# A transformer tower on one core: the sequence experts and the block attention put into one stage, piece by piece

## The chip, the cores and the metric

One core of a Trainium2 chip runs the whole program. The metric is the device time of one execution in microseconds; the median of three runs stands for a kernel. The engines are TensorE (PE), VectorE (DVE), ScalarE (ACT), GpSimd (POOL) and SyncE (SP), each with its own instruction queue that is worked off in order.

## What is computed

Eight images of 1024 tokens, 128 channels wide, pass five layers. Each adds its output to the stream `h`:

```python
h = tok(x, W) + positions
h = h + attention(layernorm(h))                 # 8 heads, softmax over 1024 keys
h = h + sequence_experts(layernorm(h))          # 2 of 8 experts for a whole image
h = h + block_attention(layernorm(h))           # below
h = h + token_experts(layernorm(h))             # 2 of 8 experts for each token

def sequence_experts(x):                        # g: gates from a pooled image, two are not 0
    h = gelu(einsum('bsd,edh->ebsh', x, w1) + b1)
    eo = gelu(einsum('ebsh,eho->ebso', h, w2) + b2)
    return einsum('ebso,be->bso', eo, g)

def block_attention(x):                         # 32 blocks of 32 tokens; all blocks are in the band
    q, k, v = x @ W_qkv + b_qkv
    attn = softmax(einsum('bisc,bjsc->bisj', qb, kb) * scale)
    out = einsum('bisj,bjsc->bisc', attn, vb)
    return out @ W_proj + b_proj
```

Block attention is within an image, and so is the gate of an image in the sequence experts. The token experts need the counts of all tokens of all images before they start.

## The kernel before

`tower` runs five blocks one after the other, with a barrier between two: `embed_and_attend` (the first two layers, 0 to 632 us of the profile), `sequence_experts` (632 to 844), `block_attention` (844 to 1155), `token_experts` (1155 to 1425), `add_results`. The stream H stays in SBUF. Between the last two the rows go through DRAM: `send` (L1580) writes the normalised rows into a queue sorted by expert.

**`sequence_experts`** (helper `expert_items`). An image takes four tiles: two halves of 512 tokens, each with two experts; 32 tiles in all. A tile has four parts n. `first` makes a hidden part in PSUM (three matmuls of 512 columns, L70 to L72, the operands split into two fp32r parts). ACT's `hidden` reads it twice with Gelu (L1192 into `g_hi`, L1195 into `g`), DVE's `low` takes the rest (L1288), `second` adds the part into `psY`. After four parts ACT's `output` makes `y` (L1208), `turn_y` transposes it into `psT` (L1257), DVE's `back` adds it to H by the gate. PE's order is `first(m + 1, n)`, then `second(m, n)`, with `turn_y(m - 1)` after n = 2. `turn_x` transposes the tokens of a new half (L1227) into `psX`, ACT (L1202) and DVE split it. All eight PSUM banks are in use: four `psH`, two `psY`, `psX`, `psT`. The class `Rest` puts what is left of the second layer and of the gates between these parts, up to tile 16. SP loads the weights of the experts.

**`block_attention`** takes image after image, over all five engines: DVE statistics and `apply_x`, PE `turn` (L1694), ACT `places` and `first_bits`, DVE `split_x`, PE `project` (L70 to L72), `values` (L1719), `scores` (L1729), DVE `shift`, ACT Exp, DVE `weights`, PE `attend` (L1741), ACT `attended`, PE `output` (L1747 to L1751), DVE `add`, statistics (L130), POOL root (L1573), `apply_z` (L141), PE `turn_z` (L1701), ACT `copy_z`, PE `logits` (L1759), DVE `choose` (two highest of 8, L1862 to L1878), PE `positions` (L1766 to L1769), DVE `route` (L1884 to L1898), POOL 16 sends. Parts of image b + 1 stand between those of b. It too uses eight banks, one or two for each purpose. After the last image comes `plan`: the counts, the tiles of each expert, the padding of the queue, four loads of weights; then the token experts' first rows are read.

## Time and profile before

| | |
|---|---|
| median of 3 runs | 1419.37 us (1413.64 to 1426.13) |
| span of the profiled execution | 1475.5 us |
| busy over the span | PE 1206.2 us (82%), ACT 994.0 (67%), DVE 932.3 (63%), POOL 557.8 (38%) |
| mean granted clock of TensorE | 0.889 |
| sequence experts | 632 to 844 us |
| block attention and plan | 844 to 1158 us |

A row of a timeline gives the start, the time (of all that a row merges), the engine, line and operation, output and inputs, how many, and in brackets how long the engine had been idle and for what. "remote" and "issue" mean that the profile shows nothing that ended the wait. Two instructions that follow each other overlap, so the cost of one is read from start to start. The clock is given in parts of the full one; 0.5 is 1.2 GHz and 1.0 is 2.4 GHz.

### The profile page before, as it was taken

The numbers are of one execution on the slowest core, as the hardware profiler recorded it, in microseconds if no ns is written. First come the engines' busy times: TensorE is split into PE (matmuls) and PEld (weight loads), VectorE is DVE, ScalarE is ACT, GpSimd is POOL, SyncE is SP. The second block draws the span as 40 slices with busy tenths as digits, with TensorE's granted clock in tenths as the row PEclk, the third lists the DMA queues.
The fourth block names the chain that finished last, engine by engine and source line by source line (L and its number), as shares of the span: only waits on it lengthen the run. The fifth ranks groups of instructions, "written<-read, shape, count | busy, mean of one in ns | idle before, by whom it ended". The sixth has DMA issues, their size and how long they took to land. (4 is left out here: it accounts for less than half of the span.)

```text
span 1475.5 us, 26945 instructions
## 1 busy us (share of the span) xinstructions
PE 1206.2 (82%) x9386; PEld 808.9 (55%) x9386; DVE 932.3 (63%) x2604; ACT 994.0 (67%) x1348; POOL 557.8 (38%) x538
## 2 busy tenths in 40 slices
PE   3699999999999998889999867877661599999950
PEld 2344444444444443477788656766451487888740
DVE  4366877777787877578676667776242266666535
ACT  0498888888888888688799744434110489999840
POOL 3423333343434332101000012667526067777660
PEclk9799999999999999899999968787555799999975
DMA  3573828282927372232122000111103467777619
GB/s 89 107 180 92 198 86 200 80 185 83 203 86 182 96 168 64 64 129 86 58 100 73 8 4 7 41 37 45 38 17 129 175 220 238 245 237 240 217 44 341
DMA packets 93162, 180.56 MB, mean 122 GB/s; under 512 B 15597, under 2 KB 64200, under 8 KB 84960
## 3 DMA queue, kind: packets, MB, share of 16 engines
q1 hardware_dynamic: 72832, 129.18, 31.3%
q0 software_dynamic: 17344, 42.68, 8.9%
q10 hardware_dynamic: 2848, 6.95, 1.7%
q8 instruction: 76, 1.25, 0.4%
q14 instruction: 62, 0.51, 0.1%
HBM read 116.96 MB, written 63.12 MB: 122 GB/s over the span
## 5 line engine op out<-in xcount | busy, mean ns | idle before, releaser
L777 ACT ACTIVATE a_probs<-a_psS 128x1024 f32<-128x1024 f32 x512 | 484.1, 1034 | 86.5 <-PE a_psS L862 53.0
L874 PE MATMUL a_psO<-a_probs,a_v 128*32 128x256 f32 x4096 | 281.6, 393 | 17.2 <-DVE a_o_t L1051 16.8
L1288 DVE TENSOR_TENSOR f_g_lo<-f_g,f_g_hi 128x512 fp32r<-128x512 f32 x284 | 194.7, 689 | 149.7 <-ACT f_g L1195 108.7
L2024 POOL DMA_INDIRECT result<-f_out,f_idx x156 | 181.4, 1163 | 107.0 <-issue 61.3
L874 PEld LDWEIGHTS a_psO<-a_probs,a_v 128*32 128x32 f32 x4096 | 108.5, 110 | 153.8 <-issue 88.8
L1580 POOL DMA_INDIRECT queue<-all_row,all_idx x128 | 125.1, 977 | 42.0 <-issue 36.9
L1192 ACT ACTIVATE f_g_hi<-f_psH,all_w 128x512 fp32r<-128x512 f32 x156 | 109.3, 701 | 24.5 <-PE f_psH L72 19.7
L1195 ACT ACTIVATE f_g<-f_psH,all_w 128x512 f32<-128x512 f32 x156 | 109.3, 701 | 0.0
L862 PE MATMUL a_psS<-ag_qs,ag_ks 50*128 50x512 f32 x512 | 97.0, 455 | 13.2 <-DMA ag_qs<-a_gparts 6.6
L862 PE MATMUL a_psS<-a_qs,a_ks 50*128 50x512 f32 x512 | 97.5, 457 | 7.7 <-issue 3.1
L438 POOL TENSOR_TENSOR ag_rs_f<-ag_veps_f,all_half 128x4 f32<-128x4 f32 x32 | 33.8, 1055 | 128.4 <-DVE ag_veps_f L135 128.4
L1202 ACT ACTIVATE f_x_hi<-f_psX 128x512 fp32r<-128x512 f32 x55 | 33.1, 602 | 59.5 <-PE f_psX L1227 59.5
L862 PEld LDWEIGHTS a_psS<-ag_qs,ag_ks 50*128 50x128 f32 x512 | 39.7, 190 | 60.9 <-ACT a_probs L777 31.0
L862 PEld LDWEIGHTS a_psS<-a_qs,a_ks 50*128 50x128 f32 x512 | 39.8, 191 | 54.9 <-ACT a_probs L777 36.7
L70 PE MATMUL f_psH<-f_x_hi,all_w 128*128 128x512 f32 x156 | 68.5, 439 | 0.0
L72 PE MATMUL f_psH<-f_x_hi,all_w 128*128 128x512 f32 x156 | 62.0, 398 | 0.0
L71 PE MATMUL f_psH<-f_x_lo,all_w 128*128 128x512 f32 x156 | 62.0, 397 | 0.0
L70 PE MATMUL f_psY<-f_g_hi,all_w 128*128 128x512 f32 x156 | 61.6, 395 | 0.0
L72 PE MATMUL f_psY<-f_g_hi,all_w 128*128 128x512 f32 x156 | 61.4, 394 | 0.0
L71 PE MATMUL f_psY<-f_g_lo,all_w 128*128 128x512 f32 x156 | 61.4, 394 | 0.0
L746 POOL DMA_DIRECT2D experts<-a_split x32 | 19.7, 615 | 107.9 <-DVE a_split L1069 107.9
L1192 ACT ACTIVATE f_g_hi<-f_psH,f_w 128x512 fp32r<-128x512 f32 x64 | 44.6, 697 | 15.1 <-PE f_psH L72 14.7
(368 smaller groups left out, 2660.0 us busy)
## 6 DMA issues: line engine op xcount, KB each, us to landing
all_w<-experts SPq DMA_DIRECT2D x39, 1026.5 KB
experts<-a_split POOLq DMA_DIRECT2D x32, 512.0 KB, 5.0
f_rows<-queue SPq DMA_DIRECT2D x39, 260.0 KB
f_w<-experts SPq DMA_DIRECT2D x8, 1026.5 KB, 5.3
qparts<-a_parts SPq DMA_DIRECT2D x16, 512.0 KB, 4.2
kparts<-a_parts SPq DMA_DIRECT2D x14, 512.0 KB, 3.3
ag_qs<-experts SPq DMA_DIRECT2D x4, 1026.5 KB, 5.1
ag_ks<-experts SPq DMA_DIRECT2D x4, 1026.5 KB, 4.8
```

The lines of the kernel that those rows point to most:

```text
L70: nc.tensor.matmul(out, w_lo, x_hi, start=first, stop=False)
L71: nc.tensor.matmul(out, w_hi, x_lo, start=False, stop=False)
L72: return nc.tensor.matmul(out, w_hi, x_hi, start=False, stop=last)
L438: self.nc.gpsimd.tensor_tensor(self.rs_f[:, :], self.veps_f[:, :], half[:, 0:TPC], ALU.pow).then_inc(self.root_f, 1)
L777: nc.scalar.activation(probs[u % NPR][:, :], psS[score_buffer(u)][:, :, :].rearrange("p a n -> p (a n)"), ACT.Exp).then_inc(exp_done, 1)
L862: last = nc.tensor.matmul(psS[score_buffer(u)][:, p, :], ks[par][64 * p:64 * p + KG, kt, hp * P:(hp + 1) * P], queries(par, hp, p, a), sta ...
L874: last = nc.tensor.matmul(psO[32 * g:32 * g + 32, a * HALF:(a + 1) * HALF], v[par][:, 2 * hp + p, kt, :], probs[u % NPR][:, cols:cols + HA ...
L1192: nc.scalar.activation(g_hi[i][:, n, :], psH[n][:, :], ACT.Gelu, bias=bias(m, n))
L1195: nc.scalar.activation(g[:, n, :], psH[n][:, :], ACT.Gelu, bias=bias(m, n)).then_inc(g_done, 1)
L1288: nc.vector.tensor_tensor(g_lo[i][:, n, :], g[:, n, :], g_hi[i][:, n, :].bitcast(F32), ALU.subtract).then_inc(lo_done, 1)
L1580: pool.indirect_dma_start(queue, bass.IndirectOffsetOnAxis(ap=idx[n % NROW][:, k, t:t + 1], axis=0), row[n % NROW][:, k, t, :], None).then ...
L2024: pool.indirect_dma_start(result, bass.IndirectOffsetOnAxis(ap=idx[i][:, j:j + 1], axis=0), out[i][:, j, :], None, bounds_check=2 * B * S ...
```

## The change

The two stages become one, `experts_and_blocks`. It counts steps: step s is part n = s mod 4 of tile m = s div 4, 16 steps to an image, 128 steps with expert work and 42 behind them. The tables of `Blocks` say at which step after the end of image b's tiles each engine does each piece of b's attention; a number in a table counts from step 16(b + 1). So pieces of three images are in flight, and in one turn of 16 steps PE meets `positions` (of b - 2), `attend`, `output` (b - 1), `turn` (b), `turn_z` (b - 1), `values`, `project0` (b), `logits` (b - 1), `project1`, `scores` (b).

PSUM is shared out anew: three `psH`, one `psY`, one `psT` (for x, y and `Rest` alike), and three banks `psB` for the attention, which go round: each use takes the bank of the use three before it and waits (`into`, `FREED`) until that one's reader is done. `turn_y` moves to n = 1. `g` is cut from four parts to three.

Smaller parts: the softmax weight of the routing is made by POOL (`route_power`), not by ACT; the copy of the rows is a DMA on SP's queue, not an activation; the bias of `output` takes one matmul of 33 rows, not two; `positions` runs in bf16; the queue's rows have two buffers, not three; SP issues the attention's constants between the expert loads. ACT's Exp (`power`) now stands among Gelus.

```diff
+class Blocks:
+    PE = {8: "turn", 10: "values", 11: "project0", 12: "project1", 13: "scores", 17: "attend", 19: "output", 26: "turn_z", 28: "logits",
+          32: "positions"}
+    ACT = {8: "places", 9: "first_bits", 10: "values", 11: "queries_keys0", 12: "queries_keys1", 14: "power", 17: "attended0", 18: "attended1",
+           26: "copy_z0", 27: "copy_z1"}
+    DVE = {3: "moments_x0", 4: "moments_x1", 6: "apply_x0", 7: "apply_x1", 9: "split_x", 14: "shift", 15: "weights", 20: "add", 21: "moments_z0",
+           22: "moments_z1", 24: "apply_z0", 25: "apply_z1", 29: "choose0", 30: "choose1", 33: "route"}
+    POOL = {5: "root_x", 23: "root_z", 31: "route_power", 34: "send0", 35: "send1", 36: "send2", 37: "send3", 38: "send4", 39: "send5", 40: "send6",
+            41: "send7"}
+    SP = {26: "copy_rows"}
+    BANKED = {"turn": ("x0", "x1"), "values": ("v0", "v1"), "project0": ("q0", "k0"), "project1": ("q1", "k1"), "scores": ("s",),
+              "attend": ("a0", "a1"), "output": ("p0", "p1"), "turn_z": ("z0", "z1"), "logits": ("l",), "positions": ("r",)}
+    STEPS = 42
+    def __init__(self, B):
+        self.B, self.end = B, 16 * B + self.STEPS
+        self.uses = [(b, name) for s in range(self.end) for b, piece in self.at(self.PE, s) for name in self.BANKED[piece]]
+        self.place = {use: u for u, use in enumerate(self.uses)}
+    def at(self, table, s):
+        return [(b, table[s - 16 * (b + 1)]) for b in range(self.B) if s - 16 * (b + 1) in table]
...
-def sequence_experts(nc, H, ident, half, mean1, rstd1, score1, gate, chosen, shared, parts, ins, B, S, D):
...
-def block_attention(nc, H, queue, counts, row, idx, sent, tile_e, tile_row, parts, w1, w1_in, ident, half, ins, B, S, D):
...
+def experts_and_blocks(nc, H, ident, half, mean1, rstd1, score1, gate, chosen, shared, experts, w, w1_in, queue, tile_e, tile_row, ins, B, S, D):
...
+    NG, NH, NBANK = 3, 3, 3
...
+        psH = [c.ps(f"psH{i}", [P, CH]) for i in range(NH)]
+        psY, psT = c.ps("psY", [P, CH]), c.ps("psT", [P, CH])
...
+        psB = [a.ps(f"psB{i}", [P, CH]) for i in range(NBANK)]
...
+        def bank(b, name):
+            return psB[plan_of.place[b, name] % NBANK]
...
+            def copy_rows(b):
+                sp.wait_ge(zn_done, b + 1)
+                sp.dma_start(row[b % NROW][:, 1, :, 0:D], row[b % NROW][:, 0, :, 0:D]).then_inc(row_in[b % NROW], 16)
...
+            copy_rows(0)
+            load_parts(4)
+            copy_rows(1)
             shared.spread_gates(sp, 1, gate, chosen)
             load_parts(5)
             sp.wait_ge(shared.gate_in, 64)
             for b in range(6, B):
+                copy_rows(b - 4)
                 load_parts(b)
+            for b in range(B - 4, B):
+                copy_rows(b)
...
+            sp.wait_ge(planned, 1)
+            sp.wait_ge(y_done, M)
+            for i in range(len(w)):
+                e = sp.value_load(tile_e[0:1, i:i + 1], min_val=0, max_val=E - 1)
+                sp.dma_start(w[i], experts[1][bass.ds(e, 1), :, :].rearrange("o p c -> p (o c)")).then_inc(w1_in[i], 16)
...
+            def send(b, lo, hi):
+                pool.wait_ge(slot_done, b + 1)
+                pool.wait_ge(row_in[b % NROW], (b // NROW + 1) * 16)
...
+                elif name == "route_power":
+                    pool.wait_ge(gap_done, b + 1)
+                    nc.gpsimd.tensor_tensor(ex[:, :], shared.base[:, 0:T], gap[:, :], ALU.pow).then_inc(ex_done, 1)
...
+            def hidden(m, n):
+                i, u = m % 2, m * NB + n
+                if n == 0:
+                    w_wait(act, m)
+                act.wait_ge(h_ps, u + 1)
+                if n == 0 and m >= 2:
+                    act.wait_ge(y_ps, m - 1)
+                nc.scalar.activation(g_hi[i][:, n, :], psH[u % NH][:, :], ACT.Gelu, bias=bias(m, n))
+                if u >= NG:
+                    act.wait_ge(lo_done, u - NG + 1)
+                nc.scalar.activation(g[u % NG][:, :], psH[u % NH][:, :], ACT.Gelu, bias=bias(m, n)).then_inc(g_done, 1)
...
+            def output(m):
+                act.wait_ge(y_ps, m + 1)
+                if m >= 2:
+                    act.wait_ge(t_ps, m - 1)
+                nc.scalar.activation(y[m % 2][:, :], psY[:, :], ACT.Gelu, bias=bias(m, NB)).then_inc(y_done, 1)
...
+                elif name == "power":
+                    act.wait_ge(sub_done, b + 1)
+                    nc.scalar.activation(pr, sc, ACT.Exp, scale=SCALE).then_inc(exp_done, 1)
...
+            for s in range(END):
+                m, n = divmod(s, NB)
+                if s == 0:
+                    act.wait_ge(c_in, C_IN)
+                if m + 1 < M:
+                    hidden(m + 1, n)
+                if n == 0 and m % K == 0 and m + K < M:
+                    token_bits((m + K) // K)
+                for b, name in plan_of.at(Blocks.ACT, s):
+                    piece(name, b)
+                if n == NB - 1 and m < M:
+                    output(m)
...
+            def first(m, n):
+                j, u = m // K, m * NB + n
+                if n == 0:
+                    w_wait(pe, m)
+                    pe.wait_ge(x_done, j + 1)
+                if u >= NH:
+                    pe.wait_ge(g_done, u - NH + 1)
+                hi, lo = first_parts(m, n)
+                product(nc, psH[u % NH][:, :], hi, lo, x_hi[j % 2], x_lo[j % 2]).then_inc(h_ps, 1)
+            def second(m, n):
+                i = m % 2
+                if n == 0 and m:
+                    pe.wait_ge(y_done, m)
+                pe.wait_ge(lo_done, m * NB + (n + 1))
+                hi, lo = second_parts(m, n)
+                last = product(nc, psY[:, :], hi, lo, g_hi[i][:, n, :], g_lo[i][:, n, :], first=(n == 0), last=(n == NB - 1))
+                if n == NB - 1:
+                    last.then_inc(y_ps, 1)
...
+            def turn_y(m):
+                pe.wait_ge(y_done, m + 1)
+                for i in range(TPC):
+                    last = nc.tensor.transpose(psT[:, i * P:(i + 1) * P], y[m % 2][:, i * P:(i + 1) * P], ident[:, :])
+                last.then_inc(t_ps, 1)
+            FREED = {"x": (xt_done, 2), "v": (v_done, 2), "q": (qk_done, 4), "k": (qk_done, 4), "s": (sub_done, 1), "a": (o_done, 2),
+                     "p": (h_done, 2), "z": (z_done, 2), "l": (sel_done, 1), "r": (slot_done, 1)}
+            def into(b, name):
+                u = plan_of.place[b, name]
+                if u >= NBANK:
+                    was, old = plan_of.uses[u - NBANK]
+                    done, each = FREED[old[0]]
+                    part = int(old[1:] or 0)
+                    pe.wait_ge(done, was * each + {"q": 2 * part + 1, "k": 2 * part + 2}.get(old[0], part + 1))
+                return psB[u % NBANK]
...
+                        out = into(b, f"p{h}")
+                        nc.tensor.matmul(out[:, :], ones_r[:, :], b_two[:, :], start=True, stop=False)
...
+                    nc.tensor.matmul(out[:, 0:TE], before[:, :], both[:, :, :], start=True, stop=False)
+                    nc.tensor.matmul(out[:, 0:TE], all_ones[:, :], counts_b[:, :].unsqueeze(1).broadcast_to([P, T, E]), start=False, stop=False)
+                    for d in range(1, T):
+                        last = nc.tensor.matmul(out[:, d * E:TE], all_ones[:, :], both[:, 0:T - d, :], start=False, stop=(d == T - 1))
...
+            for s in range(END):
+                m, n = divmod(s, NB)
+                more = m % K == 0 and m + K < M
+                if s == 16:
+                    pe.wait_ge(ready, 1)
+                    pe.wait_ge(cleared, 1)
+                if n == 0 and more:
+                    if m >= 2:
+                        pe.wait_ge(t_read, m - 1)
+                    else:
+                        pe.wait_ge(x_done, 1)
+                    turn_x((m + K) // K)
+                if m + 1 < M:
+                    first(m + 1, n)
+                for b, name in plan_of.at(Blocks.PE, s):
+                    piece(name, b)
+                if m < M:
+                    second(m, n)
+                if n == 0 and m in Rest.PE:
+                    if more:
+                        pe.wait_ge(x_done, (m + K) // K + 1)
+                    else:
+                        pe.wait_ge(t_read, m - 1)
+                    Rest.pe(shared, pe, m, psT)
+                if n == 1 and 1 <= m <= M:
+                    if m in Rest.PE:
+                        pe.wait_ge(freed, sum(m >= i for i in Rest.PE))
+                    elif more:
+                        pe.wait_ge(x_done, (m + K) // K + 1)
+                    elif m >= 2:
+                        pe.wait_ge(t_read, m - 1)
+                    else:
+                        pe.wait_ge(freed, 1)
+                    turn_y(m - 1)
+            pe.wait_ge(slot_done, B)
+            nc.tensor.matmul(psY[:, 0:E], all_ones[:, :], counts_b[:, :], start=True, stop=True).then_inc(n_ps, 1)
+        @block.vector
+        def _(dve):
...
+            def low(u):
+                m, n = divmod(u, NB)
+                i = m % 2
+                dve.wait_ge(g_done, u + 1)
+                nc.vector.tensor_tensor(g_lo[i][:, n, :], g[u % NG][:, :], g_hi[i][:, n, :].bitcast(F32), ALU.subtract).then_inc(lo_done, 1)
...
+            for s in range(END):
+                m, n = divmod(s, NB)
+                if s + 3 < M * NB:
+                    low(s + 3)
+                if n == 0 and m % 2 and (m + 3) // K < M // K:
+                    rows_next((m + 3) // K)
+                if n == 1 and m % K == 0 and m + K < M:
+                    token_rest((m + K) // K)
+                if (m, n) == (1, 2):
+                    constants()
+                rest.dve(dve, m, n)
+                for b, name in plan_of.at(Blocks.DVE, s):
+                    piece(name, b)
+                if n == 2 and 1 <= m <= M:
+                    back(m - 1)
             plan()
```

## Rows read from the trace of the kernel before

**Rows 1.** windows: stretch, us, busy us of PE, PEld, DVE, ACT, POOL; clock; DMA

```profile
641.00:844.00 203.00, 196.17 (x933) 157.97 (x931) 148.41 (x326) 174.66 (x292) 7.91 (x4) 0.99 0.19 63
...
720.00:730.00 10.00, 9.32 (x38) 7.10 (x37) 5.13 (x11) 6.62 (x11) 0.00 (x0) 0.83 0.00 2
...
966.00:993.00 27.00, 20.61 (x179) 17.75 (x179) 19.98 (x90) 11.15 (x18) 19.86 (x19) 0.81 0.12 40
```

**Rows 2.** timeline of ACT in the expert stage: start us, us, engine line op

```profile
746.08 0.69 ACT L1208 ACTIVATE f_y<-f_psY,f_w 128x512 f32<-128x512 f32 x1
...
746.81 0.69 ACT L1192 ACTIVATE f_g_hi<-f_psH,ag_ks 128x512 fp32r<-128x512 f32 x1
...
747.96 0.61 ACT L1202 ACTIVATE f_x_hi<-f_psX 128x512 fp32r<-128x512 f32 x1
...
760.46 0.61 ACT L1202 ACTIVATE f_x_hi<-f_psX 128x512 fp32r<-128x512 f32 x1
```

**Rows 3.** timeline of PE in the expert stage: one gap, first, second

```profile
718.63 0.38 PE L272 MATMUL f_psT<-ag_corr,ag_ones 128*128 128x2 f32 x2 [2.83 <-DVE all_H L1472]
...
747.26 0.40 PE L70 MATMUL f_psH<-f_x_hi,ag_ks 128*128 128x512 f32 x1
...
747.96 0.39 PE L70 MATMUL f_psY<-f_g_hi,ag_qs 128*128 128x512 f32 x1
```

**Rows 4.** timeline of PE in one attention batch at the full clock

```profile
957.87 0.49 PE L1747 MATMUL a_psO<-a_b_lo,a_ones_r 1*128 1x512 f32 x1
...
959.52 0.33 PE L1766 MATMUL a_psR<-a_both,a_before 128*128 128x64 f32 x2
...
961.45 0.48 PE L70 MATMUL a_psQ<-a_x_hi,a_w_lo 128*128 128x512 f32 x1
...
962.92 1.95 PE L1719 MATMUL a_psX<-a_w_v,a_xT 128*128 128x128 f32 x16
...
965.14 0.76 PE L1729 MATMUL a_psS<-a_k,a_q 128*32 128x32 f32 x64 [0.27 <-ACT a_k L1630]
...
965.83 1.09 PE L1694 MATMUL a_psX<-all_ident,a_f 128*128 128x128 f32 x8
```

**Rows 5.** timeline of DVE in attention: choice, half of apply, statistics

```profile
935.38 1.64 DVE L130 BATCH_NORM_STATS2 a_stat_z<-all_H 128x6 f32<-128x128 f32 x8
...
951.92 0.22 DVE L1862 TENSOR_REDUCE a_top<-a_left 128x8 f32<-128x64 f32 x1
...
953.40 0.29 DVE L1875 TENSOR_TENSOR a_both<-a_sel 128x64 f32<-128x64 f32 x1
...
954.04 1.11 DVE L141 TENSOR_SCALAR a_f<-all_H,a_mv_x,a_rs_x 128x128 f32<-128x128 f32 x4
```

**Rows 6.** timeline of POOL in attention: root, and one send

```profile
964.97 1.67 POOL L1573 TENSOR_TENSOR a_rs_z<-a_veps_z,all_half 128x8 f32<-128x8 f32 x1 [2.91 <-DVE a_veps_z L135]
...
968.24 0.96 POOL L1580 DMA_INDIRECT queue<-all_row,all_idx  x1 [0.31 <-issue]
```

**Rows 7.** timeline of ACT where its function set changes

```profile
1162.93 1.28 ACT L1192 ACT_TABLE_LOAD   x1 [0.73 <-PE f_psH L72]
...
1164.22 0.69 ACT L1192 ACTIVATE f_g_hi<-f_psH,all_w 128x512 fp32r<-128x512 f32 x1
```

**Rows 8.** timelines of PE and DVE, last attention batch to token experts

```profile
1055.26 0.56 PE L1729 MATMUL a_psS<-a_k,a_q 128*32 128x32 f32 x40
...
1074.13 0.42 DVE L1829 TENSOR_REDUCE a_mx<-a_psS 128x8 f32<-128x256 f32 x1 [20.86 <-remote]
...
1101.93 3.58 PE L1759 MATMUL a_psR<-a_w_r,a_zT 128*128 128x8 f32 x16 [0.69 <-ACT a_zT L1619]
...
1110.00 3.10 PE L1769 MATMUL a_psR<-a_both,a_all_ones 128*128 128x56 f32 x14
...
1124.32 0.23 DVE L1886 TENSOR_TENSOR a_pos<-a_psR,a_base 128x64 f32<-128x64 f32 x1 [14.76 <-remote]
...
1157.85 0.48 PE L1227 MATMUL f_psX<-all_ident,f_rows 128*128 128x128 f32 x1 [31.35 <-DMA f_rows<-queue]
```

916 lines of the change are left out of this document (428 added, 488 removed).

## The prediction

> **What bounds the kernel now.** The page comes first: no engine is busy all through, so the stages have to be read apart. The windows show the expert stage as PE's: 196 of 203 us at clock 0.99, ACT behind it with 175 [rows 1]. ACT's timeline gives its beat: two tiles from one `f_x_hi` to the next but one, 747.96 to 760.46, 12.5 us, 6.25 for a tile [rows 2]. An attention batch is the opposite: 27 us in which PE has 20.6, DVE 20.0, POOL 19.9 and ACT 11.2, at clock 0.81 [rows 1]; none is full, and each waits for the next one. Side by side the two kinds of work would fill each other's gaps.
>
> I go by one stretch, from 641 us (the tiles run) to 1157.85, the first matmul of the token experts [rows 8]: 517 us. Two holes in it belong to no work. DVE waits 20.86 us until 1074.13 for scores that began at 1055.26 and elsewhere take 0.76 for all 64 [rows 4, 8]: some 18 us. It waits until 1124.32 for `positions`, whose last matmul ends at 1113.1: 11.2 us. Both are marked "remote". The profiled span is 56 us over the median of the runs; I take it that these 29 us are part of that and that the timed runs don't have them. Their stretch is then 488 us.
>
> **What PE has to do in one turn of 16 steps.** Four tiles: 25.0 us. The pieces at the full clock, start to start [rows 4]: `turn` and `turn_z` 1.09 each; `values` 1.95; `attend` and `logits`, sixteen passes over the same weights' size, 1.9 each; four products of `project` 2 x 1.47; `scores` 0.76; `output` 2 x 1.65, less one bias matmul of 0.32 in each, 2.7; `positions` 1.93 in fp32, in bf16 some 1.0 (the trace has no bf16 one; between a quarter and all of it, 0.5 to 1.9). Sum 15.3, with the tiles 40.3 us. DVE: 148 us over 32 tiles are at most 4.6 a tile, and less without what `Rest` does, some 16 a turn [rows 1]; with 20.0 for attention 36. ACT: 175/8 + 11 = 33 and two changes of function set. POOL: sixteen sends of 1.27 and two roots of 1.67, 24 [rows 6]. So PE stays the engine with most to do, with 4 us over DVE.
>
> **What the order and the banks add.** A turn written out by hand, each engine in its queue's order, prices: `first` and `second` 0.70 each [rows 3], `hidden` 1.15, `output` 0.6, `low` 0.6, half an `apply` 1.1, statistics of a half 0.8, the rest of them 0.9 [rows 2, 5]. PE then stops at these places:
>
> - Step 3, `output` waits for `attended1`, which stands behind `hidden` of step 2: 1.0.
> - Step 8, `turn_x` waits for `back` and `turn` for `apply_x1`. DVE has `add`, 1.7 of statistics, 0.9, 1.7, two halves of apply, four `low`, `rows_next` (1.1) and `back` between step 4 and 7, 10 us from the last `output` on, PE 7.5: 2.2.
> - Step 9, `turn_y` shares `psT` with `turn_x` and waits until DVE has split x. DVE's `apply_z0` waits for `root_z`, which POOL reaches after six pairs of sends (15.2 us) and `root_x`: 1.7.
> - Step 11, `q0` gets the bank of `z1`. `copy_z1` comes on ACT after `hidden`, whose `first` PE has just done: 1.15 + 0.5 + 0.15 = 1.8.
> - Step 13, `scores` gets the bank of `logits`, free when `choose1` has made `both`. DVE has `low(s + 3)` ahead of `choose1`, and that needs the hidden part of this very step. After `first`: 1.15 + 0.6 + 1.8 (951.92 to 953.69 [rows 5]) + 0.3 of handing over = 3.8. Earlier the bank had a reader of its own.
> - Step 16, `second` waits for `y`, now in one bank. ACT has the Exp between: a load of 1.28 us, Exp 0.4, a load of 1.28 [rows 7], `hidden`, `output`. That is 6.0 after `first` of step 14 and PE has 4.0 to do: 2.0.
>
> Sum 12.5. 40.3 + 12.5 = 52.8, say 53 us a turn. Handing over from one engine to the next is an estimate, 0.1 to 0.15 each time; at nothing the turn would be 51, at 0.25 it would be 55.
>
> The clock. A gap of 2.83 us at 718.6 left a slow stretch in a stage that is else at 0.99 (0.83 over the 10 us from 720 [rows 1, 3]): 10 x 0.17 / 0.5 = 3.4 us at 1.2 GHz, 1.7 us lost. The gap at step 13 is longer. From nothing to one such loss for each of three gaps (5): I take 1. Turn: 54.
>
> One rule of the Trainium skill speaks against the change more than my rows do. Its page "ScalarE: Activation LUTs", section "What ACT_TABLE_LOAD costs", puts a switch at 1283 ns of load and some 1380 ns of drain, 2.66 us. The trace agrees on the 1283; at 1162.93 the next activation begins right behind the load, but ACT had been idle before it, so no drain could show [rows 7]. By the page two switches cost 5.3 us and not 2.6, the stop at step 16 would be 4.8 long, and the sum below 22 us higher, by estimate.
>
> **The other parts.** Tiles 0 to 3 have no attention, but every `second` with n = 0 waits for `y` of the tile before in one bank: `hidden` 1.15 and `output` 0.6 against `second` and `first`, 1.4, with handing over 0.7 a tile: 4 x 6.95 = 28. The next turn has only the pieces up to `scores` (6.7): 25 + 6.7 + three such waits, 2, + the Exp, 2 = 36. The third has no sends, so no stop at step 9: 51. Five full ones (steps 48 to 127): 270. `Rest` on one `psT`, with its additions on DVE up to tile 16: 4.
>
> Behind step 127 the last image's attention runs alone with what is left of the two before it, and PE at half clock (sixteen passes 3.58 [rows 8] for 1.95). Chain: the last `back`, `positions` and `route` of image 5, 5; four pairs of its sends 10.1 and `root_x` 1.7, at 17; meanwhile apply and turn of image 7, but `split_x` stands behind `apply_z` of image 6, whose root stands behind four more sends: 27.5; `turn_z`, `values` 5.5, `project0` 2.6, `logits` 3.6, `project1` 2.6, `scores` 1.5 and some waits for banks: 44.5; shift, load, Exp, weights 5.5: 50; `attend` 3.8, `attended` 1.1, `output` 5, `add` and statistics 3.5: 63.5, but `root_z` stands behind twelve sends of image 6, that start at 52 after `route`, so 69; apply 2.2, turn 2, copy 0.6, `logits` 3.6, `choose` 4.1, `positions` 2, `route` 2: 85.5. From `route` to the first token matmul before: 1125.8 to 1157.85, 32 (sixteen sends 20, landing, four loads of weights, rows). The same code follows: 32. Together 118.
>
> The last parts at nothing: the constants' DMAs and `constants` have SP and DVE free in the first tiles (if not, 3 us of landing once); ACT's copy of the rows goes to a DMA that is used 8 steps later; the expert loads wait on tiles of 10 us more than the transfer needs; two row buffers are enough, as the sends of b - 2 end 15 steps before `apply_z(b)`; POOL's `route_power` (about 1.7, by its roots) is needed two steps later. The barrier between the stages, 1 us, goes.
>
> Sum: 28 + 36 + 51 + 270 + 4 + 118 = 507, against 517 in the profile and 488 without the holes. The profiled execution: 1475.5 - 10 = 1466. The timed runs: 1419.4 + 19 = **1438 us**.
>
> **The rivals.**
> - *The hand order holds, but the holes are in the timed runs too and go away.* For it: the profile has them. Against: the span is 56 us longer than the runs. 1438 - 29 = 1409.
> - *The other side: PE's queue hardly stops, and the stage is bound by its work.* Mechanism: DVE and ACT run ahead, so that each piece is ready when PE comes. For it: 40.3 of work on the fullest engine, and in attention no engine is over 76% busy [rows 1], so each has room to run ahead. Against: the stops at 11, 13 and 16 are in the order itself, not in how busy an engine is. It decides at a turn of 50.5 us (19 us over five and a half turns less). At 42 to 46 with a tail of 110: 1438 - 8 x 5.5 .. - 12 x 5.5 - 8, 1386 to 1364. The Trainium skill's page "Perfetto Trace Analysis", section "Optimization Strategy", says that interleaving regimes in which different engines are fullest may gain; the windows show two such regimes [rows 1].
> - *The stops take the clock.* Three gaps of 2 us or more in 53: if PE is at half speed for a third of a turn, five to seven us are added, by the 718.6 gap's 1.7 for each and longer ones as in attention, where the clock is 0.81. 1438 + 6 x 5.5 = 1471.
> - *A change of function set costs more than its load, because ACT has to run empty first.* For it: in the one row ACT was idle before the load, so a cost of that kind could not show [rows 7]. Against: nothing in the trace has it. At most as much again as the load, 1.3 each time, twice a turn, on the path of step 16: 8 x 2.6 = 21, 1459. The Trainium skill's page named above ("ScalarE: Activation LUTs") states such a drain.
>
> **How the numbers follow.** The forecast has 0.42, the holes' rival 0.13, PE-bound 0.27, the clock 0.13, the function sets 0.05. The range leaves out the lower end of PE-bound and half of the clock's: 1366 to 1470. The likeliest's own is 1420 to 1456. Within 1% (1405 to 1434), about what a measurement of this kernel can tell, falls the lower third of the forecast and most of the second; faster by over 1% is PE-bound and a little of the second, 0.31; same 0.22; slower 0.47.
>
> **What the profile would show.** Turns of 53 to 54 us between two `project0`; PE idle 3.8 before `scores` with DVE's `choose` as releaser, 1.8 before `q0` for ACT; two table loads a turn; the token experts 118 us after the last expert matmul at a clock of 0.5. No idle before `scores`, or turns below 50, would make the forecast wrong; a mean clock under 0.9 in the turns speaks for the last rival.

## The result

The changed kernel takes 1482.7 us (median of four runs, 1480.2 to 1498.4) against 1416.5 for the kernel before beside it: ratio 1.048, 95% interval 1.042 to 1.054. With both timed again on another chip it was 1497.3 against 1421.9, ratio 1.049 (1.044 to 1.055). The forecast was 1438 us.

The profiled executions have to be set side by side with care. That of the changed kernel has a span of 1481.8 us and took 1483.9, so it is like its timed runs. That of the kernel before was 1475.5 where its runs take 1417. A second profiled execution of the kernel before, the first experiment below, has 1417.4; it is the one to compare with. All times below are counted between the starts of three matmuls: the first `first` product of the expert stage, the last expert matmul, and the first matmul of the token experts.

| us | before, first profile | before, second profile | after |
|---|---|---|---|
| first expert product starts at | 631.3 | 629.3 | 623.5 |
| from there to the score projection of `Rest` | 6.4 | 6.4 | 15.6 |
| on to the last expert matmul | 204.1 | 204.1 | 419.7 |
| on to the first token matmul | 316.0 | 264.9 | 110.3 |
| the whole stretch | 526.5 | 475.4 | 545.6 |
| behind it | 317.7 | 312.7 | 312.7 |

So all of the loss, 70 us between these executions, is in this one stretch. The windows of the changed kernel cut it by turns, from one `scores` to the next (columns: stretch, us, busy us of PE, PEld, DVE, ACT, POOL with their instructions, clock, DMA share, GB/s):

```profile
822.40:883.80 61.40, 47.41 (x287) 37.79 (x287) 37.86 (x128) 36.30 (x55) 22.80 (x19) 0.86 0.24 78
883.80:942.90 59.10, 46.27 (x287) 36.67 (x287) 36.30 (x118) 36.39 (x55) 23.52 (x19) 0.90 0.19 63
942.90:999.80 56.90, 44.01 (x287) 34.80 (x287) 36.34 (x118) 36.14 (x55) 21.37 (x19) 0.93 0.15 48
999.80:1055.30 55.50, 46.56 (x277) 37.56 (x277) 32.66 (x109) 33.57 (x51) 21.50 (x20) 0.84 0.10 29
```

A turn takes 55 to 61 us, 54 were forecast. No engine is full, and the clock is 0.84 to 0.93, where the expert stage of before has 0.99 and an attention batch 0.81 [rows 1] (0.86 in the second profile). The turns repeat: in a second execution (e15) these four are 61.4, 59.1, 57.0 and 55.5. The waits of PE in the second of these turns (engine, line waited for: us, times, longest):

```profile
PE a_psB L1750 <- DVE a_both L1962: 4.0, 1, 4.0
PE f_psY L70 <- ACT f_y L1590: 2.6, 1, 2.6
PE a_psB L70 <- ACT a_zT L1633: 1.9, 1, 1.9
PE f_psT L1674 <- DVE all_H L1863: 1.6, 1, 1.6
PE f_psT L1700 <- DVE ag_ks L1848: 1.3, 1, 1.3
PE a_psB L1766 <- ACT a_oT L1626: 1.0, 1, 1.0
PE a_psB L1733 <- DVE ag_n L1888: 0.3, 1, 0.3
```

These are the stops of the forecast, one by one, with their releasers (sum 12.7; 12.6 to 14.3 in the other four of the five turns from the second `scores` to the seventh). The chain behind the longest is visible on DVE: `low` waits for the hidden part of this very step, then comes `choose1`, and `scores` starts with the `both` that it makes.

```profile
881.27 0.69 DVE L1854 TENSOR_TENSOR f_g_lo<-f_g,f_g_hi 128x512 fp32r<-128x512 f32 x1 [2.27 <-ACT f_g L1580]
882.06 0.22 DVE L1949 TENSOR_REDUCE a_top<-a_left 128x8 f32<-128x64 f32 x1
...
883.54 0.22 DVE L1962 TENSOR_TENSOR a_both<-a_sel 128x64 bf16<-128x64 f32 x1
```

What the forecast lacks stands behind the stop, in PE's timeline (start us, us, engine line, operation; in brackets the idle time before and its releaser):

```profile
883.92 1.08 PE L1750 MATMUL a_psB<-a_k,ag_res 128*32 128x32 f32 x64 [3.98 <-DVE a_both L1962]
...
885.52 0.63 PE L71 MATMUL f_psY<-f_g_lo,ag_ks 128*128 128x512 f32 x1
...
888.08 0.63 PE L72 MATMUL f_psH<-ag_qs,all_w 128*128 128x512 f32 x1
...
889.17 0.39 PE L72 MATMUL f_psY<-f_g_hi,ag_ks 128*128 128x512 f32 x1
```

For some 4.6 us, 883.92 to 888.5, each `first` or `second` matmul takes 0.63 us and not 0.39, 0.43 and not 0.23 from start to start: half speed, and over 2 us lost, behind a stop of 4. And ACT shows the start of the stage, where the expert work waits for a constant that only attention needs:

```profile
636.41 0.69 ACT L1577 ACTIVATE f_g_hi<-f_psH,ag_ks 128x512 fp32r<-128x512 f32 x1 [5.23 <-DMA ag_pe_tab<-b_proj]
```

### The profile page after: what moved, and what is told of

Its sections match the earlier page's. It is cut to its first block and busy times, and to the rows that moved or that the text cites. A ratio compares the mean times of both kernels' runs of the same rounds, so it can differ in the third digit from the quotient of the medians.

```text
span 1481.8 us, 26888 instructions
## 1 busy us (share of the span) xinstructions
PE 1180.9 (80%) x9297; PEld 777.5 (52%) x9297; DVE 932.1 (63%) x2612; ACT 1005.9 (68%) x1346; POOL 582.0 (39%) x548
## 5 line engine op out<-in xcount | busy, mean ns | idle before, releaser
L827 PE MATMUL a_psO<-a_probs,a_v 128*32 128x256 f32 x4096 | 277.7, 389 | 17.1 <-DVE a_o_t L1004 16.7
L1525 POOL DMA_INDIRECT queue<-a_row,a_idx x128 | 132.8, 1037 | 121.8 <-DVEq L1986 86.5
L815 PE MATMUL a_psS<-ag_qs,ag_ks 50*128 50x512 f32 x512 | 96.5, 453 | 14.3 <-DMA ag_qs<-a_gparts 7.4
L1577 ACT ACTIVATE f_g_hi<-f_psH,all_w 128x512 fp32r<-128x512 f32 x64 | 44.0, 687 | 52.4 <-PE f_psH L72 44.7
L70 PE MATMUL f_psY<-f_g_hi,all_w 128*128 128x512 f32 x140 | 59.1, 422 | 8.8 <-ACT f_y L1590 8.5
L1537 POOL TENSOR_TENSOR a_ex<-ag_base,a_gap 128x8 f32<-128x8 f32 x8 | 13.3, 1666 | 128.5 <-DVE a_gap L1963 128.5
L1143 ACT ACTIVATE f_g_hi<-f_psH,all_w 128x512 fp32r<-128x512 f32 x76 | 53.1, 698 | 10.0 <-PE f_psH L72 9.2
L71 PE MATMUL f_psY<-f_g_lo,all_w 128*128 128x512 f32 x140 | 56.6, 404 | 0.0
L72 PE MATMUL f_psY<-f_g_hi,all_w 128*128 128x512 f32 x140 | 56.4, 403 | 0.0
L1153 ACT ACTIVATE f_x_hi<-f_psX 128x512 fp32r<-128x512 f32 x39 | 23.5, 601 | 45.2 <-PE f_psX L1178 45.2
L1146 ACT ACTIVATE f_g<-f_psH,all_w 128x512 f32<-128x512 f32 x76 | 53.0, 698 | 0.0
L1178 PE MATMUL f_psX<-all_ident,f_rows 128*128 128x128 f32 x156 | 24.4, 281 | 34.3 <-DMA f_rows<-queue 31.1
```

What stands on the lines that cost most here:

```text
L70: nc.tensor.matmul(out, w_lo, x_hi, start=first, stop=False)
L71: nc.tensor.matmul(out, w_hi, x_lo, start=False, stop=False)
L72: return nc.tensor.matmul(out, w_hi, x_hi, start=False, stop=last)
L815: last = nc.tensor.matmul(psS[score_buffer(u)][:, p, :], ks[par][64 * p:64 * p + KG, kt, hp * P:(hp + 1) * P], queries(par, hp, p, a), sta ...
L827: last = nc.tensor.matmul(psO[32 * g:32 * g + 32, a * HALF:(a + 1) * HALF], v[par][:, 2 * hp + p, kt, :], probs[u % NPR][:, cols:cols + HA ...
L1143: nc.scalar.activation(g_hi[i][:, n, :], psH[n][:, :], ACT.Gelu, bias=bias(m, n))
```

## Experiments

In short (the stretch is from the first expert product to the first token matmul in the run's profile; a turn is the mean of the five from the second `scores` to the seventh; ratio to the kernel before on the same chip):

| run | time us | ratio (95%) | stretch | turn |
|---|---|---|---|---|
| after | 1482.7 | 1.048 (1.042 to 1.054) | 545.6 | 58.7 |
| e1 newest first on PE, ACT | 1444.0 | 1.015 (1.012 to 1.018) | 501.2 | 50.9 |
| e2 stop filled, 16 matmuls | 1491.7 | 1.051 (1.048 to 1.054) | 536.5 | 56.2 |
| e3 Identity for Exp (softmax left out) | 1474.3 | 1.037 (1.034 to 1.040) | 532.6 | 56.8 |
| e4 in sequence | 1572.0 | one run | 627.5 | |
| e5 newest first everywhere | 1441.8 | 1.017 (1.012 to 1.021) | 500.1 | 51.0 |
| e6 and a later Exp | 1418.3 | 1.000 (0.997 to 1.003) | 470.4 | 47.4 |
| e7 two banks for y | 1483.4 | 1.048 (1.042 to 1.054) | 534.9 | 56.6 |
| e9 e6, constants waited for later | 1410.9 | 0.993 (0.990 to 0.996) | 464.1 | 47.4 |
| e10 stop filled, 8 matmuls | 1490.7 | 1.048 (1.044 to 1.052) | 538.9 | 57.3 |
| e11 e9, DVE's pieces ahead of `low` | 1403.9 | 0.986 (0.983 to 0.990) | 460.2 | 47.4 |
| e12 after with that alone | 1468.1 | 1.032 (1.028 to 1.036) | 519.6 | 54.6 |
| e13 e11 with a stop added | 1447.0 | 1.016 (1.014 to 1.019) | 501.3 | 52.4 |
| e14 that stop filled | 1434.3 | 1.008 (1.005 to 1.012) | 485.2 | 50.6 |
| e15 after, second profile | 1505.5 | one run | 551.2 | 59.5 |
| e16 after, timed again | 1497.3 | 1.049 (1.044 to 1.055) | 553.6 | 59.5 |
| e17 e2, beside e16 | 1483.6 | 1.048 (1.043 to 1.052) | 540.1 | 56.2 |
| e18 e7, beside e16 | 1478.7 | 1.041 (1.037 to 1.045) | 535.1 | 57.3 |

### What the kernel before really takes in the stretch (e0)

No edit.

> The kernel before, unchanged, for a second profiled execution. The prediction's accounting: the 59 us by which the first profiled execution of before lay over the timed runs are in two holes (29 us) and in places that the change doesn't touch (30 us); then a profile whose span is near 1415 shows 641 to the first token matmul as some 488 us. Rival: all 59 us lie in that one stretch; then it is 458 to 462 us long, the stages ahead of it and behind it are as before (641, 264, 54), and the forecast for the timed runs should have been 1466 by its own sum of 507. Third: this execution too is near 1475, and the profiler itself costs it.

1419.4 us, span 1417.4. The rival holds: 475.4 us from the first expert product to the first token matmul (466 counted from where the prediction starts; the rival had 458 to 462), 51 less than in the first profile, while 6.4, 204.1 and the time behind are within 5 us of it. Some 27 of the 51 are behind the last `scores`, where the holes were; the other 24 are ahead of it: half of them in the last batch, and the batches before take 23.9 us and not 27 [rows 1]:

```profile
933.00:956.90 23.90, 19.96 (x180) 17.68 (x179) 19.67 (x87) 11.48 (x17) 19.16 (x19) 0.86 0.14 46
```

The first hole was not empty as the prediction has it. The row at 1055.26 [rows 8] has 40 of the 64 `scores`; the other 24 come one to five at a time over the next 12 us (first profile):

```profile
1059.66 0.32 PE L1729 MATMUL a_psS<-a_k,a_q 128*32 128x32 f32 x3 [1.17 <-issue]
...
1067.55 0.21 PE L1729 MATMUL a_psS<-a_k,a_q 128*32 128x32 f32 x1 [1.19 <-issue]
```

In the second profile all 64 take one row of 0.78 us. Why the first profiled execution was so much slower in attention alone isn't known; no timed run was.

### The two halves of the change, apart (e4)

```
-        return [... table[s - 16 * (b + 1)] ... for b in range(self.B) ...]
+        return [... table[s - 16 * (b + 8)] ... for b in range(self.B) ...]
```

and SP issues all `load_parts` ahead of `copy_rows`.

> After with the pieces of all attention batches moved behind the last expert tile (the same tables, 16 steps an image, the same banks; the loads of experts and the copies of rows put in the order that this needs). Prices the two halves of the change apart. From the stretch's first matmul to the last expert matmul the kernel before takes 204.1 us. Theory 'the one bank for y and three for the hidden parts cost 0.7 a tile': 204 + 22 + 4 for the rest of the gates = 225 to 232. Rival: they cost nothing, 204 to 208. Behind it the attention in this order alone: after's tail shows scores 43 us apart at image 7; 38 to 43 us an image against 24 in the kernel before, in its undisturbed execution, as a chain of DVE, PE and POOL steps in one order. Then the stretch is 225 + 8 x 40 + 60, some 600 us, and the interleaving does gain 70 against its own pieces; what loses is the order. If an image takes 24 to 28 here too, the order costs nothing and the interleaving is what loses.

Experts and one attention batch:

```profile
645.30:877.20 231.90, 212.08 (x943) 159.70 (x944) 151.99 (x328) 178.25 (x291) 7.74 (x4) 0.98 0.16 55
1019.00:1060.90 41.90, 21.39 (x167) 18.14 (x167) 19.82 (x89) 10.70 (x15) 21.16 (x19) 0.63 0.12 39
```

The stretch is 627.5 us, where some 600 were expected. The new PSUM share costs the experts 27.8 us (231.9 against 204.1; the forecast's 0.7 a tile and 4 for `Rest` make 26). The order of the pieces, with one image at a time and three banks, takes 42 us for a batch that took 24. A turn of after, 58.7, is 12 below 29 + 42: the interleaving does gain. But the kernel before has 25.5 + 23.9 = 49.4. The change buys overlap with a form of attention that is 18 us longer and a form of the experts that is 3.5 us longer.

### The order inside a step (e1, e5, e12)

e1: in a step with two pieces, PE and ACT take the newer image's first.

```
+        order = range(self.B - 1, -1, -1) if table in (self.PE, self.ACT) else range(self.B)
+        return [(b, table[s - 16 * (b + 1)]) for b in order if ...]
```

> After, with PE and ACT taking the newer image's piece first where one step has two (steps 10 and 12 of a turn): the bank of q0 is then freed by the copy of v1, that of scores by the copy of q1, and both stops go that waited for copy_z1 (1.9 us) and for choose1 (4.0 us). Theory 'the stops take the clock' (PE's turn of 59.1 us is 40.4 of work, 12.7 of stops, 5.9 of matmuls at half speed behind them): two stops and the slow stretches behind them go, 5.9 + 4 = 10 us a turn, 2 or 3 of it used up by new waits at steps 10 and 12; 7 turns, so 50 to 60 us: 1425 to 1435, mean clock in the turns 0.95 and over. Rival 'PE's work was priced too low and the clock is only a by-product': 5.9 a turn, less new waits, 25 to 35 us: 1450 to 1458. Rival 'another engine bounds the turn anyway': under 10 us.

1444.0 us, 39 less, from two lines. That is between the first two theories. The waits for `both` and, but for 0.3, for `z` are gone; the turn is 7.8 us shorter where the two stops were 5.9. That is more than the stops and less than the first theory's 10: the clock in e1's turns is 0.90 to 0.97, and `turn_x` now waits up to 2.9 for `back`.

e5 puts DVE and POOL in that order too, and `back` ahead of the pieces of its step.

> The first reordering (1444 us, turns of 51.2) taken further: newest image first on DVE and POOL too (split_x ahead of the half of apply_z, root_x and root_z ahead of a pair of sends), and DVE's back ahead of the step's pieces. It aims at the stops of PE that are left there: turn_x behind back 2.9, turn_y behind split_x 1.3, y 1.6, attended 1.0. Theory 'stops and their clock set the turn': 2.9 + 1.3 go, with the clock 5 us a turn: turns of 46 to 47, 1410 to 1418, and root_z earlier gives the tail 2 to 4 us: 1408 to 1416. Rival 'a stop that is taken away comes back at the next place, as DVE works 36 to 38 us of a turn' (the run without the function sets gave 13 us in the stretch where 28 were expected, and its stop at turn_x rose from 1.6 to 3.6): 1 to 2 us a turn, 1430 to 1438.

1441.8, within 3 of e1: the rival, and 4 above its number. In the turn 879.9 to 930.6 of e1 PE stops 2.6 for `back`, 1.3 at `turn_y`, 1.5 for `y` and 0.3 for `apply_x1`. In e5 these are 0, 0, 2.8 and 2.1:

```profile
PE f_psY L70 <- ACT f_y L1590: 2.8, 1, 2.8
PE a_psB L1733 <- DVE ag_n L1888: 2.1, 1, 2.1
PE a_psB L1766 <- ACT a_oT L1626: 1.0, 1, 1.0
```

The stops moved along the chain; the sum of these four fell only from 5.7 to 4.9.

e12 is after with one edit on DVE, `low(s + 3)` at the end of a step and not at its start.

> After with that one edit: on DVE each step's pieces ahead of low(s + 3). The prediction put 3.8 us of the stop at scores to choose1 standing behind low(s + 3). Theory: without it choose1 begins when choose0 of the step before is done, its 1.8 us run while PE does second and first, and 3 to 4 of the 4.0 us go, as do parts of those at turn_x and turn_y; with the clock 6 to 8 us a turn: 1430 to 1440. Rival 'DVE is short of time as a whole, so whatever goes first, something else is late': 1470 to 1480.

1468.1, a ratio of 1.032 for after's 1.048, and nearer to the rival's number than to the theory's. Of the 4.0 at `scores` 2.6 go (1.4 left), of the 1.6 at `turn_x` 1.1; `y`, `z` and `attended` wait as before. So `choose1` behind a `low` that waits for the hidden part of its step was most of that stop, not all: what is left is the chain from `logits` on, `choose0`, one `low` and `choose1`, 4.1 us from 932.46 to the end of `both`.

### The Exp and its two loads (e3, e6, e7, e18)

e3: `ACT.Identity` in place of `ACT.Exp`.

> After, with Identity in place of Exp (the softmax is left out: the weights are the shifted scores over their sum; all else the same), so that ACT needs no change of function set. Prices the two loads of 1.28 us a turn and the stop of 2.6 us at step 16. Theory 'the stops take the clock': 2.6 and 1.5 to 2 of clock a turn, 7 turns, and 2.6 in the tail: 1445 to 1455. Rival 'only the stop itself': 18 + 3: 1460 to 1463. Rival 'a change costs a drain of 1.4 us beside each load': then the stop would shrink by over 4 us a turn with the clock on top, 1435 or less; after's rows show the loads start 0.03 us behind the activation ahead of them, which speaks against it.

1474.3, less gain than either of the first two theories. The 2.6 for `y` are gone, but

```profile
PE f_psT L1674 <- DVE all_H L1863: 3.6, 1, 3.6
```

was 1.6 (in a turn of 58.1): PE comes to `turn_x` sooner and DVE's `back` isn't ready. Of 2.6 taken away 2.0 came back one wait later; against that `turn_y` waits 0.3 and no longer 1.3, and the mean turn is 1.9 shorter. After's own rows settle the third theory:

```profile
889.33 0.68 ACT L1580 ACTIVATE f_g<-f_psH,all_w 128x512 f32<-128x512 f32 x1
890.04 1.28 ACT L1646 ACT_TABLE_LOAD   x1
891.33 0.42 ACT L1646 ACTIVATE a_pr<-a_sc 128x256 f32<-128x256 f32 x1
891.77 1.28 ACT L1577 ACT_TABLE_LOAD   x1
893.06 0.69 ACT L1577 ACTIVATE f_g_hi<-f_psH,all_w 128x512 fp32r<-128x512 f32 x1
```

The load begins 0.03 us after the activation ahead of it ends, and the next activation 0.01 after the load: 1.28 us each way, with no drain of its own.

e6 is e5 with the Exp, and what follows it, two to three steps later, `turn_z` behind `scores`:

```
-    PE = {..., 13: "scores", 17: "attend", 19: "output", 26: "turn_z", 28: "logits", 32: "positions"}
+    PE = {..., 13: "scores", 19: "attend", 21: "output", 29: "turn_z", 31: "logits", 35: "positions"}
-    ACT = {..., 14: "power", ...}     DVE = {..., 15: "weights", ...}
+    ACT = {..., 16: "power", ...}     DVE = {..., 17: "weights", ...}
```

> The same with the Exp two steps later (behind the hidden part of step 16 and not ahead of y), and all behind it, with turn_z behind scores, two to three steps later, so that neither y nor a bank waits for the two loads of a function set. Theory 'stops and their clock': the 1.6 + 1.0 that are left go, another 3 us a turn: turns of 43 to 44, 1390 to 1400 (below the kernel before); the tail longer by nothing, since it is a chain and not a count of steps. Rival 'comes back elsewhere': within 5 us of the run above.

1418.3, level with the kernel before: 23.5 less than e5 and 18 above what the first theory had put; the second, 5 at most, falls. In the turn below no `y` and no bank waits for a load any more. What came in exchange is small, 1.2 for `diag`, and with some 6 us of stops the clock stays up in this turn (0.93 to 1.00 in all five):

```profile
854.60:901.80 47.20, 41.01 (x289) 32.37 (x287) 35.85 (x117) 35.70 (x55) 20.93 (x19) 1.00 0.23 78
```

This window also gives PE's work in a turn at full clock: 41.0 us.

e7 is after with `NH` 2 and two banks for `y`.

> After, only with PSUM shared otherwise: two banks for y and two for the hidden parts in place of one and three. The stop of 2.6 at step 16 goes; in exchange first waits for the hidden part of two steps before. Theory 'the one bank for y matters, and two hidden banks are enough as ACT needs 1.15 for each and PE 1.4': 3 to 4 us a turn and 0.5 a tile elsewhere, 1455 to 1465. Rival 'ACT's two loads then stop first instead': within 5 us of after, 1478 to 1488, with the stop of PE at f_psH <- f_g and not at f_psY.

1483.4, equal to after's first timing, but its stretch was 11 us shorter than after's. On another chip, beside after (e18):

> After with two banks for y and two for the hidden parts. In the profile the stretch was 11 to 16 us shorter than after's two. Theory 'the one bank costs': 8 to 14 us below after beside it. Rival 'nothing': within 4 us.

1478.7 (1472.3 to 1486.1) against 1497.3 (1478.9 to 1501.4): the two banks do gain, 19 us by the medians, 12 by the two ratios. A stop of 1.0 to 1.3 at `first` takes the place of 2.6 at `y`, and `turn_y` waits up to 2.5. Against a time from another chip, as in e7, that gain can't be seen.

### The constants (e9)

```
-                if s == 0:
+                if s == 24:
                     act.wait_ge(c_in, C_IN)
```

> The late-Exp order (1418.3 us) with ACT's wait for the constants' transfers moved from step 0 to step 24, where attention first reads them. From the first hidden matmul of the stage to the first matmul of the score projection the changed kernels take 15.6 to 15.9 us, the kernel before 6.4; ACT waits 5.2 there for b_proj. The prediction had this part at nothing, 3 at most. Theory 'the constants stop ACT at the start': 5 to 9 us less, 1409 to 1413, and ACT's row of 5.2 goes. Rival 'the start is late for something else' (the loads of experts share the queue): within 2 us.

1410.9, 7.4 less than e6. From the first product to the projection it is 11.0 instead of 15.5 us, and ACT's row of 5.23 is gone. The kernel before takes 6.4; of what is left PE waits 3.77 for `f_x_lo`, since the projection now needs the bank `psT` that `turn_x` filled.

### Does a stop take the clock? (e2, e10, e17, e13, e14)

e2 puts work that nobody reads into the 4.0 us before `scores`:

```
                 elif name == "scores":
+                    if b < B - 1:
+                        pe.wait_ge(t_read, 4 * b + 6)
+                        for i in range(16):
+                            nc.tensor.matmul(psT[:, :], w_hi[:, 0, :], bx_hi[:, 0:CH], start=True, stop=True)
```

> After, with 16 superfluous matmuls (their result is read by nobody) on PE in the stop before scores, so that PE works through the 4.0 us in which it waited for choose1. No wait is shortened. Theory 'the stops take the clock': the 5 us at half speed behind this stop go, 2 to 2.5 us a turn, 7 turns: 1465 to 1470, and the matmuls behind scores take 0.40 instead of 0.63. Rival 'the clock falls for the power or the load of the whole and not for that stop': no gain, or a loss as the added work heats it: 1483 to 1490.

The profiled execution has turns of 54.9 and 54.0 at clock 1.00 for 59.1 and 56.9, yet the median was 1491.7, just above the rival's range (the profiled execution, 1479.2, was the fastest of the five). With 8 (e10):

> The run with superfluous matmuls ahead of scores again, with 8 instead of 16. Of the 16, the profiled execution had turns 3.5 us shorter at clock 1.00, but the timed ones 1489 to 1496 against 1480 to 1498: at half speed 16 take 6.9 us, more than the stop of 4.0, and then delay scores. 8 take 1.9 us at full speed and 3.4 at half, so they fit either way. Theory 'a stop of 4 us costs half speed behind it, one of 2 does not': 2 to 3 us a turn, 1462 to 1470. Rival 'the clock falls also for the short stop': within 3 us of 1483.

1490.7, above both theories, though the stretch was 7 us shorter than after's. And beside after on one chip (e16, e17):

> The changed kernel itself, beside the two below and the kernel before. If the other chips' hours don't matter: 1480 to 1486, ratio 1.045 to 1.050. If the stage ahead is as late as in the other executions of changed code (first hidden matmul at 628 to 639 us and not at 623.3): 1488 to 1500, ratio 1.052 to 1.058.

> After with 16 superfluous matmuls in the stop before scores. Theory 'idling takes the clock', with the pair of the added stop (12.7 us between empty and filled): 7 to 13 us below after beside it. Rival: filling a stop of 4.0 with matmuls that last 3.7 at full and 6.9 at half speed gains in some turns and loses in others: within 4 us of after.

After 1497.3 (1478.9 to 1501.4), filled 1483.6 (1480.7 to 1498.0): 13.7 less in the median, but ranges that overlap, and the ratios, 1.049 and 1.048, are level. So the times alone don't decide. The turns do: the four shown in the section on the result (822.4 to 1055.3) take 232.8 to 233.1 us together in all three profiles of after (e15 and e16 too) and 219.0 and 219.2 in those of e2 and e17, with every other wait of the turn from 883.8 equal to 0.2. That is 3.5 a turn given back by filling one stop of 4.0; with 8 matmuls (e10) it is 225.3. Ahead of the first `scores` the filled kernels take 3 to 6 us more. A second pair is e13 and e14, in the fastest order, whose turns run at a clock of 0.96 to 1.00. e13 adds a stop, by a piece of ACT in step 13 and a wait of PE ahead of `scores`; e14 puts 14 such matmuls ahead of that wait:

```
+                elif name == "halt":
+                    act.wait_ge(p_ps, b * 2)
+                    nc.scalar.activation(oT, bxT, ACT.Identity)
+                    act.drain()
+                    last = nc.scalar.activation(oT, bxT, ACT.Identity)
+                    last.then_inc(halt, 1)
...
+                    pe.wait_ge(halt, b + 1)
```

> The fastest order so far (1403.9 us, turns of 47 at clock 0.97 to 1.00), with one stop added in each turn: ACT does two superfluous activations of 1024 elements (their result is written over before it is read) behind the hidden part of step 13, and PE's scores wait for them, some 3.5 us. Theory 'a stop of this length costs half speed behind it': 3.5 and 2 to 2.5 of clock a turn, 8 times: 1445 to 1450, clock in the turns 0.90 to 0.95. Rival 'the stop costs only itself': 1428 to 1432 with the clock at 0.97 to 1.00. Third: it takes up slack that waited at the next place anyway: 1410 to 1420.

> The same added stop, filled with 14 superfluous matmuls on PE (3.2 us at full speed), so that only the engine's idling is taken away, not the wait. Theory 'idling takes the clock': the 2 to 2.5 us a turn are not lost: 15 to 20 us less than the run with the empty stop, clock at 0.97 to 1.00. Rival: no difference beyond 5 us.

1447.0 (1446.3 to 1451.1) and 1434.3 (1426.4 to 1437.3). Two turns of each, empty above, filled below:

```profile
868.90:922.00 53.10, 43.36 (x287) 34.45 (x287) 35.55 (x117) 37.25 (x58) 21.61 (x19) 0.94 0.22 68
922.00:974.00 52.00, 42.34 (x287) 33.60 (x287) 35.52 (x117) 37.31 (x58) 22.03 (x19) 0.96 0.19 64
```

```profile
853.00:903.60 50.60, 43.97 (x301) 34.93 (x301) 35.45 (x117) 37.27 (x58) 21.59 (x19) 1.00 0.24 73
903.60:954.00 50.40, 44.08 (x301) 34.96 (x301) 35.52 (x117) 37.23 (x58) 22.03 (x19) 1.00 0.19 63
```

The wait is in both (3.4 us in e13; e14's mean turn is 3.3 longer than e11's; all other waits of the turn are equal to 0.1); only PE's idling differs. It costs 2.5 and 1.6 us in these turns, 16 over the stretch (501.3 against 485.2), 12.7 in time. The stop took the clock: with its own length, 3.4, it cost 5.1 a turn (501.3 against the 460.2 of the same order without it, e11, over eight turns), filled 3.1.

### How far one execution is from another (e15)

> The changed kernel, unchanged, for a second profiled execution: from the first hidden matmul of the stage to the first token matmul the first one took 545.6 us. If one execution is like another, 541 to 550 and turns of 57 to 61; if the filled stop's 7 to 9 us are only such a difference, this one may be at 535 to 540. The stage ahead (first hidden matmul at 623.3 us, in nine others of the changed code at 628 to 638) is expected later than in the first, at 630 to 637.

1505.5 us, the stretch 551.2, just over what was expected. The turns repeat to 0.1 us from the third on; the first two differ by 1.6 and 4, and the unchanged stage ahead ended at 639.6 against 623.5. The executions of changed code have it anywhere in between. So two times of changed code from different chips or hours can't be told apart below 10 to 15 us. A profiled stretch is better, but it too has a spread of 8 us in after (545.6, 551.2, 553.6), and the kernel before had 526.5 and 475.4; what repeats to 0.3 is the sum of the third to the sixth turn.

### The version that beats both (e11)

> The run with the constants' wait moved, and on DVE in every step the pieces, back, rows_next and token_rest ahead of low(s + 3), which is due only three steps later. Left in the turns of 47 to 48 us are the stops at turn behind apply_x1 0.8 to 1.6, at turn_y behind token_rest 1.3, at attend behind weights 1.2 to 2.3, sum 4 to 6; all three stand behind a low that waits for a hidden part just begun. Theory 'pieces that stand behind low': 3 of them go, 3 to 4 us a turn: 20 to 25 us less than the run above, 1385 to 1395. Rival 'low comes late instead and second or hidden stops': no gain or a loss, and the stop moves to f_psY behind f_g_lo.

1403.9 us (1398.0 to 1409.3), 1.4% faster than the kernel before on the same chip; 7 less than e9, where 20 to 25 were expected. The stop at `turn` fell from 1.6 to 0.8, but `second` now waits 1.3 for `y`, where it didn't wait: the turn is 47.0 for 46.9. What gain there is in the profile, 3.9 us, lies ahead of the first `scores` (72.8 us from the first product on, where e9 has 76.3), not in the turns. Its stretch, 460.2, is 15 below that of the kernel before.

## Why the prediction was wrong

The sign was right and so was the list of what PE waits for; three sizes were off, in this order.

**The holes.** "Their stretch is then 488 us" fails. The profile's surplus of 56 us was taken as 29 in two holes and the rest elsewhere; 51 of it lay in this stretch, since besides the holes a batch of attention took 27 there and 23.9 in the second execution. Counted as the prediction does (from 9.7 us behind the first expert product) the kernel before takes 475.4 - 9.7 = 466. With that, its own 507 gives 1419.4 + 41.3 = 1461 us. These are 22 of the 45 us missed. Of a surplus of 56 us the step had placed 29 and left 27 without a place; that remainder was the warning. That the holes "belong to no work" was also misread for the first, in which PE still had 24 `scores` to do. The rival "the holes are in the timed runs too" falls with it.

**The clock.** "I take 1" fails. PE is busy 46.3 in the turn from 883.8 and 41.0 in a turn of e6 at clock 1.00: 5.3 a turn, not 1. Over the five turns of the table it is some 4.4 in the mean (58.7, less 41.0 of work and 13.3 of stops). The rival "the stops take the clock" had the mechanism and nearly the size (five to seven us, 1471), and the pairs e13 and e14, e16 and e17 show it; its sign, a mean clock under 0.9 in the turns, came with 0.89. The price taken from [rows 3], 1.7 lost behind a gap of 2.8, was about right for one gap (2.0 behind the added 3.4, though 3.5 behind the 4.0), and three of them were the bound of 5 that the step itself named; what failed is that it took 1 of those 5.

**The parts at nothing.** The constants' transfers were put at nothing, 3 at most, as SP and DVE are free there. Both are; ACT is not. Its wait for all of them stands at step 0, ahead of the first tiles' hidden parts: 9.2 us more than before to the projection, of which e9 gives back 4.5 (7.4 in time); most of the rest is the wait for the shared `psT`, for which the prediction had 4 with all of `Rest`. The question that the change of a wait asks (who is queued behind it) was put for every stop in the turn and not for this one.

**What held.** The six stops, forecast and measured in the turn from 883.8: step 3, 1.0 and 1.0; step 8, 2.2 and 1.9; step 9, 1.7 and 1.3; step 11, 1.8 and 1.9; step 13, 3.8 and 4.0; step 16, 2.0 and 2.6; sum 12.5 and 12.7. PE's work 40.3 and 41.0. DVE 36 and 36.3, POOL 24 and 23.5, ACT 33 and two loads, together 35.6, and 36.4. The turn: 40.3 + 12.5 + 1 = 54 forecast, 41.0 + 12.7 + 5.3 = 59.0 measured. The PSUM share of the experts, 26 and 27.8. The tail, 118 and 110.3, 8 too long; PE's longest wait in its attention, 12.0 us ahead of the last `turn_z`, is the one that was named, `root_z` of the last image behind twelve sends of the image before:

```profile
1119.51 0.95 POOL L1525 DMA_INDIRECT queue<-a_row,a_idx  x1 [0.31 <-issue]
1120.48 1.67 POOL L1534 TENSOR_TENSOR a_rs_z<-a_veps_z,all_half 128x8 f32<-128x8 f32 x1
```

Sum over the stretch: 507 forecast, 545.6 - 9.7 = 536 measured, 29 more: 9 at the start, 28 in the turns, 8 less in the tail. With the 22 of the holes that is 51, and 45 were missed: the stage ahead ended 5.8 us earlier in this execution than in the second profile of before, which is luck and not part of the forecast.

**The other rivals.** PE-bound: no turn with expert tiles in it was below 55, and it decided at 50.5. It is what e6, e9 and e11 come near to, 47 us for 41 of work, and only in e9 and e11 does the change gain. The drain at a change of the function set: e3's small gain and the rows above speak against it. For this the Trainium skill's page "ScalarE: Activation LUTs", section "What ACT_TABLE_LOAD costs", gives 1283 ns of load and some 1380 of drain; the trace agrees with the 1283 and shows 0.03 us in place of the drain, so here the measurement decides. The Trainium skill's "Perfetto Trace Analysis", section "Optimization Strategy", says that interleaving regimes whose most contended engine differs may improve the performance: e4 against after shows that gain, 12 us a turn, and that it didn't pay for the rest.

## What to carry to other kernels

Before two stages are laid over each other, price each of them alone in the form that the overlay needs (fewer banks, one image at a time): here 29 + 42 us against 25.5 + 23.9, and the overlay had to win back 22 before it won anything. A stop of PE can cost more than its length (5.1 us for 3.4 in e13), so price an order that has several of 2 to 4 us in a turn at more than their sum; look for them where a ring of banks makes a matmul wait for the slowest reader, and try first which of two pieces in the same step goes first (39 us for two lines). A stop that is taken away from one place often comes back at the next wait of the same chain; read the waits again before the gain is booked.

## What was not expected of the hardware

- A stop of 3.4 us on PE cost 1.6 to 2.5 us beyond itself in the two turns shown; after one of 4.0 the matmuls took 0.63 us for 4.6 us and then 0.39 again. In the fifteen turns of e6, e9 and e11, with 4 to 7 us of stops and none over 2.5, the clock was 1.00 in eight.
- A stop isn't all that can take it. In the turn of e9 from 749.9 to 799.7 the clock was 0.90 with no stop over 1.5 us: half speed begins at 758.6, behind the sixteen short matmuls of `logits`, with a wait of 0.44 us ahead of them. What took it there wasn't tested:

```profile
755.49 1.95 PE L1782 MATMUL a_psB<-a_w_r,a_zT 128*128 128x8 f32 x16 [0.44 <-ACT a_zT L1633]
...
758.81 0.63 PE L71 MATMUL f_psH<-ag_ks,all_w 128*128 128x512 f32 x1
```

- A load of a function set between two busy stretches of ACT costs its 1.28 us and no more.
- A profiled execution can be 4% longer than the timed runs, 1475.5 us for 1417, with nearly all of it in one stretch (526.5 for 475.4).
- What stays open: why that execution was slow, why the stage ahead, the same instructions, ends between 623.5 and 639.6 us in changed code, and how much of e2's, e10's and e17's shorter turns is in their times.
